# A fused cross-attention and feed-forward layer: another order of the attention turn and of the change of half, streamed weights fetched from ScalarE's queue

## What is computed

```python
x = x + tanh(g_xattn[0]) * xattn(layernorm(x), ctx_2048, ...)   # q = rms_norm(linear(x)), k = rms_norm(linear(ctx)), softmax(q k / sqrt(32)) v, linear
x = x + tanh(g_ffn[0]) * ffn(layernorm(x), ...)
# ffn: h = square(relu(z @ up)); y = h @ down + (z @ expert_weight) * sum(top_2(z @ gate_w)); layernorm(y) * gamma + beta
```

## Time and profile before

| | us |
|---|---|
| median of 3 runs (1451.42 to 1457.24) | 1451.87 |
| the profiled execution | 1454.03 |
| its span, first to last instruction | 1452.2 |
| TensorE (PE) busy | 1364.3 |
| VectorE (DVE) busy | 942.7 |
| ScalarE (ACT) busy | 595.0 |
| GpSimd (POOL) busy | 524.4 |

### The profile page before, as it was taken

The page is one execution under the profiler, slowest core; times in us unless marked ns, Lnnn a source line. Parts: engine busy times, 40 slices in busy tenths (PEclk is TensorE's granted clock), DMA queues, the critical chain, the costliest instruction groups (busy, mean ns, idle before and its releaser), DMA issues.

```text
span 1452.2 us, 28145 instructions
## 1 busy us (share of the span) xinstructions
PE 1364.3 (94%) x9264; PEld 1145.4 (79%) x9264; DVE 942.7 (65%) x1765; ACT 595.0 (41%) x1863; POOL 524.4 (36%) x673
## 2 busy tenths in 40 slices
PE   6799999999999988989999999999999999999996
PEld 4677777777777777779888888789888888888895
DVE  4555555556666656479687577577686785775854
ACT  3666666666666665643231221212312312312120
POOL 2455555555555445664213014013022130140121
PEclk9899999999999999999999999999999999999998
DMA  6123333333332140135754845746738549458540
GB/s 219 51 87 101 97 100 98 100 98 105 102 101 79 59 126 29 37 116 189 194 170 143 239 151 149 222 138 177 228 124 213 185 131 244 145 149 239 169 152 29
DMA packets 215090, 199.15 MB, mean 137 GB/s; under 512 B 126320, under 2 KB 126448, under 8 KB 215024
## 3 DMA queue, kind: packets, MB, share of 16 engines
q1 hardware_dynamic: 214448, 197.26, 45.2%
q10 hardware_dynamic: 576, 1.05, 0.2%
HBM read 156.32 MB, written 41.94 MB: 137 GB/s over the span
## 4 chain that ended last, share of the span: by engine, by line
PE 36%; issue 19%; POOL 17%; DVE 8%; DMA 7%; SPq 6%; ACT 2%; POOLq 0%; DVEq 0%; ACTq 0%
PE bank L75 7%; PE bank L77 7%; PE bank L76 7%; POOL prob L783 6%; SPq L1398 4%; DMA xn_scratch<-fx 4%; PE wide L76 3%; PE wide L75 3%; PE wide L77 3%; POOL eight L770 2%; DMA wo_lo<-ring_scratch 2%; POOL xres L805 2%; PE bank L291 1%; POOL fy L971 1%; PE wide L306 1%
## 5 line engine op out<-in xcount | busy, mean ns | idle before, releaser
L1550 ACT ACTIVATE hT_hi<-c 128x512 fp32r<-128x512 f32 x128 | 79.9, 631 | 403.0 <-PE wide L77 218.7
L625 ACT ACTIVATE prob<-wide,nmx 128x128 f32<-128x128 f32 x512 | 181.9, 402 | 104.1 <-DVE nmx L459 100.9
L1777 POOL TENSOR_TENSOR pair<-pair,beta 128x512 f32<-128x512 f32 x28 | 39.2, 1401 | 463.4 <-DMA pair<-x_scratch 463.4
L76 PE MATMUL wide<-wo_lo,hT_hi 128*128 128x512 f32 x512 | 203.3, 397 | 0.0
L77 PE MATMUL wide<-wo_hi,hT_lo 128*128 128x512 f32 x512 | 201.9, 394 | 0.0
L75 PE MATMUL wide<-wo_hi,hT_hi 128*128 128x512 f32 x512 | 201.6, 394 | 0.0
L783 POOL TENSOR_TENSOR prob<-prob,rr 128x512 f32<-128x512 f32 x128 | 137.9, 1088 | 146.2 <-DVE rr L467 146.2
L1623 DVE TENSOR_TENSOR hT_lo<-c,hT_hi 128x512 fp32r<-128x512 f32 x128 | 99.4, 796 | 77.2 <-ACT hT_hi L1550 77.1
L625 ACT ACTIVATION_READ_ACCUMULATOR prob<-wide,nmx 128x1 f32 x512 | 124.3, 243 | 0.0
L77 PEld LDWEIGHTS wide<-wo_hi,hT_lo 128*128 128x128 f32 x512 | 96.1, 188 | 22.7
L75 PEld LDWEIGHTS wide<-wo_hi,hT_hi 128*128 128x128 f32 x512 | 96.2, 188 | 21.7
(11 more groups left out here) (230 smaller groups left out, 3656.3 us busy)
## 6 DMA issues: line engine op xcount, KB each, us to landing
wo_hi<-ring_scratch SPq DMA_DIRECT2D x156, 256.0 KB, 3.0
wo_lo<-ring_scratch SPq DMA_DIRECT2D x156, 256.0 KB, 3.4
fx<-x_scratch SPq DMA_DIRECT2D x36, 256.0 KB
xin<-in_x SPq DMA_DIRECT2D x32, 256.0 KB, 2.6
cin<-in_ctxT SPq DMA_DIRECT2D x32, 256.0 KB, 2.8
xres<-in_x SPq DMA_DIRECT2D x32, 256.0 KB, 3.9
x_scratch<-x SPq DMA_DIRECT2D x32, 256.0 KB, 3.0
out_x<-fy SPq DMA_DIRECT2D x32, 256.0 KB
```

The source lines that it names most:

```text
L76: eng.matmul(dst, ah, bl, start=False, stop=False)
L625: i = act.activation(prob[par][:, g, h * P:(h + 1) * P], cols(bank[g], h), ACT.Exp, bias=nmx[:, n:n + 1], scale=1.0, accum_out=rs[:, n:n + 1])
L1550: return act.activation(dst, src, ACT.Copy)
L1777: pool.tensor_tensor(res(g, j), res(g, j), ff.beta[:, :], ALU.add).then_inc(ff.po_r, 1)
```

## The change

On TensorE, the query projection moves up directly behind the key projection, the output projection moves behind three groups of transposed probabilities and waits for `qb` (bank 7 must be read first), all four groups of values come behind the transposition of kf, and `turn_x` gets a wait for the residual sum, since bank 7 holds the output projection until then. On VectorE, the first reciprocal moves ahead of `kb`, `qb` ahead of `kf`, and the residual sum behind `qf`. On ScalarE `square_q` moves ahead of three copies of probabilities. On GpSimd the third division moves ahead of rk, and mq and rq move ahead of the residual and the context split.

The loads for the second half are spread over the ends of slots 23 to 27, the first tiles are normalised in slots 24 to 27, sums of tiles and weights are made in slots 28 to 30, into buffers of their own (`tsum`), and the first up weights are split at the end of slot 30. The drain has a new order, in which VectorE makes two of each four copies of transposed probabilities, and the first transpositions of the feed-forward rotate over more banks. In the feed-forward, ring loads n = 4 to 17 are issued by ScalarE: two a quarter behind `copy_1` and `copy_5`, and n = 16 and 17 behind the last two hidden copies of the group. SyncE keeps n = 18 and 19 and the next group's first four.

```diff
-                return b - (NB - 5) if isinstance(b, int) and NB - 5 <= b < NB - 1 else None
+                return b - (NB - 8) if isinstance(b, int) and NB - 8 <= b < NB - 4 else None
...
-                    if is_slot(s, NB - 5):
-                        for m in range(2):
-                            sp.wait_ge(st_x2[m], GB // 2 * DMA)
-                        ff.load_first(sp)
...
+                    if is_slot(s, NB - 9):
+                        for m in range(2):
+                            sp.wait_ge(st_x2[m], GB // 2 * DMA)
+                    if isinstance(s, int) and NB - 9 <= s < NB - 4:
+                        ff.load_first(sp, s - (NB - 9))
...
+                    at_least(pe, dv_x2, b - 3)
...
                         mm3(pe, BK, cT[1 - par], wk, ready=split_weight(n, 0)).then_inc(pe_K, 1)
-                    if has(o):
                         at_least(pe, dv_xT, n + 1)
-                        project_out(o, BO)
-                    if has(a):
-                        turn_probs(a, 1 - par, 0)
-                        turn_probs(a, 1 - par, 1)
-                        turn_probs(a, 1 - par, 2)
-                    if has(n):
-                        at_least(pe, dv_xT, n + 1)
-                        at_least(pe, dv_x2, o + 1)
                         mm3(pe, BQ, xT, wq, ready=split_weight(n, 1)).then_inc(pe_Q, 1)
                     if is_slot(s, 0):
                         pe.wait_ge(dv_vb, 1)
                         mm3(pe, BV, cT[1 - par], wv).then_inc(pe_V, 1)
                     if has(a):
+                        turn_probs(a, 1 - par, 0)
+                        turn_probs(a, 1 - par, 1)
+                        turn_probs(a, 1 - par, 2)
+                    if has(o):
+                        at_least(pe, dv_qb, n + 1)
+                        project_out(o, BO)
+                    if has(a):
                         turn_probs(a, 1 - par, 3)
-                        values(a, 1 - par, 0)
                     if is_slot(n, 0):
                         keep_clock(BV, 4, D)
                     if has(n):
                         at_least(pe, dv_kf, n + 1)
-                        at_least(pe, ac_pT, a * NG + 3)
+                        if has(a):
+                            probs_taken(pe, a, 2)
                         turn(kf, BTK, pe_Tk)
                     if is_slot(n, 0):
                         keep_clock(BV, 8, D)
                     if has(a):
-                        values(a, 1 - par, 1)
-                        values(a, 1 - par, 2)
-                        values(a, 1 - par, 3)
+                        for g in range(NG):
+                            values(a, 1 - par, g)
...
+                    pe.wait_ge(dv_x2, o)
                     project_out(o, BO)
-                    turn_probs(a, a % 2, 0)
-                    turn_probs(a, a % 2, 1)
-                    turn_probs(a, a % 2, 2)
+                    for g in range(NG):
+                        turn_probs(a, a % 2, g)
+                    probs_taken(pe, a, 1)
+                    ff.turn(pe, 0, t_first)
+                    for g in range(NG):
+                        values(a, a % 2, g)
+                    ff.turn(pe, 1, t_first)
+                    ff.turn(pe, 2, t_first)
+                    ff.turn(pe, 3, t_first)
                     pe.wait_ge(dv_x2, o + 1)
-                    ff.turn(pe, 0, t_first)
-                    turn_probs(a, a % 2, 3)
-                    values(a, a % 2, 0)
-                    values(a, a % 2, 1)
-                    values(a, a % 2, 2)
-                    ff.turn(pe, 1, t_first)
-                    values(a, a % 2, 3)
+                    project_out(a, BO)
...
+                def take_probs(a, g):
+                    at_least(dve, pe_TP, a * NG + (g + 1))
+                    src = (BTP_LAST if is_slot(a, NB - 1) else BTP)[g]
+                    dve.tensor_scalar(pT[:, g, :], src, 0.0, None, ALU.add).then_inc(dv_p, 1)
...
                             maxima(s, g)
+                        inverse(s, 0)
...
                         inverse(s, 2)
-                    if has(o):
-                        residual_sum(o, par, BO)
+                    if has(n) and has(s):
+                        at_least(dve, pe_Q, n + 1)
+                        dve.tensor_tensor(as_strips(qb[:, :]), as_strips(BQ), by_strip(bq[:, :]), ALU.add).then_inc(dv_qb, 1)
...
+                    if has(o):
+                        residual_sum(o, par, BO)
...
+                        ff.split_gate_lo(dve)
+                        for m in range(3):
+                            ff.up_lo(dve, 0, m)
...
+                    square_q(n)
+                    if has(a):
                         take_probs(a, 1)
                         take_probs(a, 2)
                     if has(n + 1):
                         hi_ctx(n + 1, par)
                     if has(a):
                         take_probs(a, 3)
-                    square_q(n)
...
+                    divide(s, par, 2)
                     if not is_slot(s, 0):
                         inv_rms_k(n)
-                    divide(s, par, 2)
                     divide(s, par, 3)
+                    inv_rms_q(n)
+                    if has(a):
+                        residual(a, 1 - par)
                     if has(n + 1):
                         lo_ctx(n + 1, par)
-                    if has(a):
-                        residual(a, 1 - par)
-                    inv_rms_q(n)
+                    if is_slot(s, NB - 4):
+                        ff.up_sums(pool, 0)
+                    if is_slot(s, NB - 3):
+                        ff.x_sums(pool, 0, 0, t_first)
                     if is_slot(s, NB - 2):
-                        ff.up_sums(pool, 0)
+                        ff.x_sums(pool, 0, 1, t_first)
...
-    T_FIRST = (("x", 0), ("x", 2), ("x", 1), ("t", 0), ("x", 3), ("t", 1), ("t", 2), ("t", 3))
-    T_BANK = (7, 7, 7, 6, 7, 6, 6, 7)
+    T_FIRST = (("x", 0), ("x", 1), ("t", 0), ("t", 1), ("t", 2), ("t", 3), ("x", 2), ("x", 3))
+    T_BANK = (5, 6, 4, 5, 6, 4, 7, 7)
...
+    def ring_load(eng, g, n):
+        at_least(eng, ff.pe_R, g * NS + (n - KT + 1), apart=eng is nc.sync)
+        i = n if is_last(g) else ff.ring_order[n]
+        for m in range(2):
+            eng.dma_start(ff.ring[n % KT][m].bitcast(F32), ring_dram[i, m]).then_inc(ff.ring_moved[n % KT], DMA)
...
                     out_blocks(g + 1, i)
-                if q > 0 and 2 * q + 2 < (NI if last else NS):
-                    ring_load(g, 2 * q + 2, last)
                 for i in moved:
                     in_blocks(g + 1, i)
-                if q > 0 and 2 * q + 3 < (NI if last else NS):
-                    ring_load(g, 2 * q + 3, last)
...
+                if q > 1:
+                    ring_load(act, g, 2 * q)
+                    ring_load(act, g, 2 * q + 1)
...
+            ring_load(act, g, NI)
+            ring_load(act, g, NI + 1)
```

164 lines of the change are left out of this document (78 added, 86 removed).

## The result

| | before | changed |
|---|---|---|
| median of the runs, us | 1453.84 (1451.42 to 1457.24, 4 runs) | 1415.97 (1413.96 to 1417.17, 4 runs) |
| profiled execution, us | 1454.03 | 1416.72 |
| its span | 1452.2 | 1414.9 |

The ratio is 0.9736, 95% interval 0.971 to 0.9763: 37.9 us faster by the medians, 37.3 by the two profiled executions. Forecast were 43.5 of the profiled time and 1408 for the median. (The median before was 1451.87 when the forecast was made; a fourth run, of 1455.82, moved it to 1453.84.)

A forecast was written before the change was run, and what follows sets the result against it. TensorE, busy 94% of the span, bounds the kernel, so only its waits or lower-clock stretches can go: 21+6.5+3+5+8 = 43.5 off the profiled 1454.0 gives 1410.5, as a median 1408; range 1386 to 1428.

The forecast's parts named there:

- the second rival: Feed-forward: it gains nothing or loses because the third expert load lands late; 1416 to 1421, chance 0.12.
- qf held by the residual: Attention slot: GpSimd's residual holds qf until T+13.00, the sum behind it ends T+13.67, period 17.52 instead of 18.23.
- The period of TensorE's own work: Attention slot: TensorE's work without waits takes 16.90; a new 0.62 wait before xn makes the period 17.52.
- the first rival: Attention slots: qf passes before the residual and the xn wait vanishes, 17 us less, 1389; chance 0.13.
- sign of a wait of 0.5 to 0.7 before xn: Attention slot: a 17.5 slot would show this TensorE wait, released by the residual sum.
- Twenty-eight slots give 19.9: Attention: 0.71 less in each of twenty-eight slots; with slot 30's whole 1.33, 21 us together.
- Slot 27: Attention slot with a late xres: spreading the second half's loads over slots 23 to 27 gains 6.5 us (0 to 6.6).
- Start 3: Slot 1: without its 2.60 wait for qf and the lower clock after it, 3 us gained (0 to 5).
- Change of half 5: From 607.5 to 632.5: earlier operand sums and copies shared by VectorE gain 5 us of 8 (-2 to 8).
- Feed-forward 8: Feed-forward: ring loads issued by ScalarE remove waits and a low-clock stretch, 8 us of 8.5 (-5 to 10).
- no half clock after slot 1: Sign for the whole kernel: TensorE shows no stretch at half clock after slot 1.
- so no copy is behind them: Feed-forward: ScalarE issues ring loads after both copies; only a hidden-block copy over 5 us later follows, issues under 2.

The follow-up runs named there:

- run 1: Changed kernel with GpSimd's residual made to wait for qf: 1388.02 us, ratio 0.9561 to the kernel before.
- run 2: Changed kernel with the residual sum ahead of qf on VectorE: 1385.54 us, ratio 0.9536 to the kernel before.
- run 3: Changed kernel with the attention's loop written out: 1409.58 us, ratio 0.9704 to the kernel before.
- run 5: Changed kernel with all loads for the second half issued together at the end of slot 23: 1421.78 us, ratio 0.9787 to the kernel before.
- run 9: Kernel before with only GpSimd's order changed (residual, mq and rq, then context split behind qf): 1437.72 us, ratio 0.9896 to the kernel before.
- run 6: Changed kernel with the low parts of the second product's weights ahead of the squares in VectorE's drain: 1413.62 us, ratio 0.9733 to the kernel before.
- run 4: Changed kernel with the ring loads back in SyncE's program between stores and reloads: 1423.78 us, ratio 0.9807 to the kernel before.
- run 8: Changed kernel with the ring loads ahead of the two copies in ScalarE's program: 1428.57 us, ratio 0.9825 to the kernel before.

## Why the prediction was right, and where it was off

The time came out within 8 us of the forecast and the main mechanism as forecast. Part of the closeness is luck: the terms that were 8.65 too large are offset by 2.5 in terms that were too small, and one small term came about in another way than forecast. Against the forecast went that the profiled execution had the longest feed-forward of the six with the same instructions. 1416 is also what the second rival gave. Its mechanism, an expert load that lands late, did not happen: the change has no wait for the ring.

**qf held by the residual: right, to the hundredth.** Forecast were the residual at T+11.42, qf to T+13.00, the sum to T+13.67, a period of 17.52. Measured in slot 20: 11.45, 13.02, 13.68, 17.54. kf at 0.75 instead of 1.52 was right too. Slot 24 and runs 1 and 2 show the cause from three sides: the residual late, the residual made to wait, the sum taken from behind qf.

**The period of TensorE's own work: wrong, without effect here.** I took 16.90 unheld; it is 16.55, since the new order has the transposition of kf ahead of the values and no longer between two parts of them. The wait before xn was therefore 0.95, not 0.62; the slot did not change, because the other chain set it. But it is why the repair was worth 28 to 30 us (runs 1 and 2), and why the first rival's 1389 was near to what that way gives: 1388 and 1385.5. Most of the 0.35 lies in that place: from the fourth group of transposed probabilities to xn it is 2.27 in slot 20 before and 1.97 in slot 24 of the change. The forecast's sign of a wait of 0.5 to 0.7 before xn was missed for this reason.

**"Twenty-eight slots give 19.9": the largest step that failed.** I took slot 20, which is written out, for all, as in the kernel before the loop's slots differ by 0.07 at most. Once the chain of exponentials, divisions and inverse roots sets the slot, what the loop adds lies on it: 17.81 and 18.05. That is 5.8 in fourteen slots (run 3), in slots 3 to 16. Slot 24 gave 1 back.

**Slot 27: right.** Forecast 6.5; it now takes 17.55, and run 5 brings the loss back in another slot (7.2 in that slot, 5.8 by the median). The reason that I gave, the spreading, is what run 5 shows. What a late xres holds is another thing than before, though: the context split behind it, and no longer qf.

**Start 3: the number near, the reason wrong.** Of the 3.72, 1.41 come before slot 0, where the ten other runs with the same start differ by as much (32.1 to 33.8, against 32.06 here and 33.47 before). Slots 0 and 1 gained 2.3. The waits of 2.60 for qf and of 0.89 for kb in slot 1 are gone, but two for ScalarE's copies of probabilities took their place, of 2.27 and 1.02 where before there had been one of 1.06:

```profile
59.47 0.65 PE L340 MATMUL bank<-ident,prob 128*128 128x128 f32 x4 [2.27 <-ACT pT L621]
```

The stretch at the lower clock did not go either: the slot's mean granted clock is 0.81, against 0.82 before, and the transposition of qf takes 0.93. I had asked only what leaves when qf comes earlier. Run 9, which keeps TensorE's old order, gained more at the start, 5.8.

**Change of half 5: too small,** 6.78, inside its bounds. The waits of 1.25, 2.88 and 1.20 that the old drain had for weight and operand parts fell to one of 0.86, and the mean granted clock rose from 0.93 to 1.00.

**Feed-forward 8, measured 3.35: one term too small, two losses left out.** The stretches with ring waits gained 10.5, not 8.5. Lost were 3.85 from the first product to quarter 2 of group 0, of which 2.31 are the wait at the second product (run 6): I had said that VectorE does its weight splits "in front of the second product" and had not asked what GpSimd runs at that time. The sign "no half clock after slot 1" was missed there: 3.4 us at 1.2 GHz. Lost were 3.4 more in waits for the sum. Of these about 1.2 are the step "so no copy is behind them" gone wrong: in group 0 the high parts of the up weights are behind the issues, 1.56 later than with the loads in SyncE's program (run 4). The other 2.2, in groups 1 to 6, are not shown to be a property of the change: from group 0's quarter 2 to the end the profiled execution took 790.8, and the five others with the same instructions 786.6 to 789.5. What makes those transfers land later in one execution than in another stays open.

**The Trainium skill's rule on the port** ("SBUF — State Buffer", section "SBUF: two separate sides") I had read too narrowly. It names operations of VectorE in a two-port mode beside those with two inputs in SBUF. The rows bear out that one input can be enough. qf has one input, in SBUF, takes 0.49 alone and is held; the copy of probabilities out of PSUM, the same operation and size, takes 0.68, and 0.69 out of another bank:

```profile
L506 DVE TENSOR_SCALAR pT<-bank x2: 692/692/692, 585.4 to 587.0; 128x512 f32<-128x512 f32 x2
L506 DVE TENSOR_SCALAR pT<-wide x2: 683/683/683, 594.9 to 596.1; 128x512 f32<-128x512 f32 x2
```

(That is the view of one line: ns min/median/max, first and last start.) The residual sum, with one input in PSUM, took 0.74 beside the split. The Trainium skill's same page, in its section "Who interferes with whom", counts `tensor_scalar`, qf's operation, among those that can enter a two-port mode; no run here shows the mode itself.

**The Trainium skill's rule on issuing engines** ("DMA: Bandwidth & Descriptors", section "Issuing engines are not separate DMA queues"), by which only issue time is saved, would have given 1416 by the forecast's terms, with no gain in the feed-forward. Runs 4 and 8 show two things beside transfer time that the issuer decides: what a load waits behind in program order (7.9 us in the stretches), and what waits behind the load (12.6 us, and 1.2 in group 0 even in the better place).

**The new order of TensorE itself** brought nothing in the slots as they stand: run 9, with the old one, has slots as short. It pays once the sum no longer waits (runs 1 and 2), when 17.54 becomes 16.55; with the old order the slot's own work is 16.9 by the working of the prediction, an estimate that no run tested.

## What to carry to other kernels

When an operation is held at a port that another engine took first, look at what is queued behind it before shortening it: putting the sum ahead of the held qf (run 2) gained as much as freeing qf (run 1), without a new wait. Cost a chain in the looped part and in the part written out separately as soon as another chain comes to bound it. And when a queue's work moves to a compute engine, place it behind what the next engine wants soonest: the same loads in the same program cost 12.6 us more when they stood two copies earlier. Ask it for every group: in the first one another copy stood behind them, and it cost 1.2. And before a difference of a few us in waits is put down to an edit, look at other executions of the same instructions: here such waits came to between 2.9 and 7.0.

## What the runs showed of the hardware that I had not expected

- A single-input operation of VectorE from SBUF to SBUF was held for nearly the whole of GpSimd's in almost every slot: 1.46 on average over 32 instead of 0.49. It ended 0.29 after GpSimd's operation, as in the earlier trace rows.
- The hold works the other way too: the context split took 1.43 on average in the changed kernel and 1.29 with qf out of its way (run 1). A sum of 128x256 on VectorE took 2.23 beside an operation of 2.41 on GpSimd, and 0.42 elsewhere.
- Standing in a hardware loop cost 0.28 and 0.52 a slot in turn in the changed kernel, and 0.00 and 0.07 in the kernel before, where another chain set the slot.
- Four load issues on ScalarE (in the changed kernel 0.33 to 1.17 each, median 0.41 and 0.45) cost TensorE 11.3 us of named waits when they stood ahead of a copy. Behind it they cost none that the profile names as theirs; through the copies of up weights behind them in group 0 they made one wait for VectorE's sum 1.2 longer.
